# Two layers of cross-attention on one core: early weights behind the next unit's rows, a compact key table, and later copies of value products

## The reference

```
x = attn8(ln(x), ln(x)) + x            # 16 heads of 16; q, k, v and probabilities rounded to 8 bits
x = attn8(ln(x), context) + x          # the same, 77 keys
x = (a * gelu(g)) @ w2 + x             # a, g = halves of ln(x) @ w1, 1024 wide
# second layer
q, k, v = rms(x) @ Wq, rms(context) @ Wk, rms(context) @ Wv    # 16 query heads, 4 key heads of 64
x = softmax(rope(q) rope(k)^T / 8 + mask) v @ Wo + x
x = (silu(x @ Wgate) * (x @ Wup)) @ Wdown + x
```

## Time and profile before

| what | value |
| --- | --- |
| median of 3 runs | 2611.18 us (2611.0 to 2615.15) |
| profiled execution | 2606.43 us |
| its span | 2604.6 us |
| mean granted clock of PE | 0.872 |
| busy: PE, DVE, ACT, POOL | 77%, 69%, 44%, 36% |
| DMA, mean over the span | 96 GB/s |

### The profile page before, as it was taken

How to read it: one execution, slowest core, us unless ns; L and a number is a source line. 1 busy time by engine, 2 the same in 40 slices (tenths; PEclk the granted TensorE clock), 3 DMA queues, 4 the chain that set the end, 5 groups by cost and what they waited for, 6 DMA issues and landing times.

```text
span 2604.6 us, 41636 instructions
## 1 busy us (share of the span) xinstructions
PE 2006.9 (77%) x10552; PEld 1439.3 (55%) x10552; DVE 1807.6 (69%) x3327; ACT 1137.0 (44%) x1906; POOL 944.2 (36%) x1628
## 2 busy tenths in 40 slices
PE   3556477978788787888788787878787787878786
PEld 2323255655556565656556565656555565656665
DVE  1456768677777868677877868677777868685532
ACT  1234453545344553545454554545353545444211
POOL 1213334344443434343443434343433424343212
PEclk8666688999989898998989898998889898989888
DMA  7577453453636353443536363543545353634010
GB/s 234 114 133 145 90 120 73 82 123 75 129 73 133 63 123 74 97 106 74 130 73 132 65 135 61 104 99 74 121 73 124 66 130 60 129 60 105 9 40 4
DMA packets 749785, 251.18 MB, mean 96 GB/s; under 512 B 661244, under 2 KB 742896, under 8 KB 749360
## 3 DMA queue, kind: packets, MB, share of 16 engines
q1 hardware_dynamic: 746287, 249.54, 45.6%
q10 hardware_dynamic: 3328, 0.01, 0.1%
HBM read 88.62 MB, written 22.40 MB: 43 GB/s over the span
## 4 chain that ended last, share of the span: by engine, by line
PE 39%; DVE 18%; issue 16%; SPq 12%; ACT 6%; DMA 5%; POOL 3%; DVEq 1%; ACTq 0%; POOLq 0%
PE work L1389 17%; PE work L1399 14%; SPq L541 4%; DMA PT<-Pn 3%; ACT E L894 3%; DVE scaled_row L1050 3%; PE rowps L1460 3%; DVE Pn L1057 2%; PE outps L1445 2%; DVE hids L1197 1%; POOL scs L794 1%; SPq L532 1%; DVE st L1073 1%; DMA xa<-in_x 1%; DVE xs L1187 1%
## 5 line engine op out<-in xcount | busy, mean ns | idle before, releaser
L1050 DVE TENSOR_SCALAR_CACHE_REDUCE scaled_row<-rowps,der 128x1024 uint8<-128x1024 f32 x512 | 654.6, 1279 | 322.8 <-PE rowps L1460 322.6
L894 ACT ACTIVATE E<-rowps,ebias,der 128x1024 f32<-128x1024 f32 x512 | 615.2, 1203 | 405.0 <-DVE scaled_row L1050 311.4
L1057 DVE TENSOR_SCALAR Pn<-E,rowinv 128x1024 int16<-128x1024 f32 x512 | 390.9, 764 | 164.1 <-DMA PT<-Pn 140.1
L728 POOL TENSOR_TENSOR rowden<-rowsum,raw 128x1 f32<-128x1 f32 x512 | 118.7, 232 | 957.5 <-ACT E L894 956.2
L1460 PE MATMUL rowps<-KC,QP 16*128 16x512 bf16 x1024 | 219.7, 426 | 242.1 <-ACT E L894 232.1
L731 POOL TENSOR_TENSOR rowinv<-rowden,minus 128x1 f32<-128x1 f32 x512 | 332.0, 648 | 91.6 <-POOL rowden L728 91.6
L1460 PEld LDWEIGHTS rowps<-KC,QP 16*128 16x128 bf16 x1024 | 49.0, 92 | 410.6 <-ACT E L894 281.6
L1389 PE MATMUL work<-hTs,ff_w_sb 128*128 128x256 f32 x1024 | 263.8, 413 | 13.0 <-ACT hTs L870 13.0
L1389 PEld LDWEIGHTS work<-hTs,ff_w_sb 128*128 128x128 f32 x1024 | 204.6, 206 | 60.4 <-issue 16.0
L1554 PE MATMUL work<-K,hids 128*128 128x154 f32 x1024 | 156.3, 305 | 28.8 <-DVE scs L1211 18.8
L1554 PEld LDWEIGHTS work<-K,hids 128*128 128x128 f32 x1024 | 141.4, 194 | 46.2 <-DVE scs L1211 25.1
(11 more groups left out here) (142 smaller groups left out, 3281.2 us busy)
## 6 DMA issues: line engine op xcount, KB each, us to landing
VW<-vw_dram SPq DMA_DIRECT2D x32, 640.0 KB, 4.8
K<-k_dram SPq DMA_DIRECT2D x16, 616.0 KB, 4.2
KC<-k_dram SPq DMA_DIRECT2D x128, 64.0 KB, 2.4
VB<-v_dram SPq DMA_DIRECT2D x64, 128.0 KB, 3.2
PT<-Pn SPq DMA_TRANSPOSE x512, 3.1
V<-v_dram SPq DMA_DIRECT2D x16, 320.0 KB, 3.9
vw_dram<-scs SPq DMA_DIRECT2D x32, 154.0 KB
K<-k_dram SPq DMA_DIRECT2D x16, 308.0 KB, 3.1
```

The source lines that it names most:

```text
L728: nc.gpsimd.tensor_tensor(rowden[:, n:n + 1], rowsum[:, n:n + 1], raw[:, DW1:DW1 + 1], ALU.mult).then_inc(row_den.sem, 1)
L894: nc.scalar.activation(E[:, slot, :], rowps[n % 2][:], ACT.Exp, bias=ebias[:, n:n + 1], scale=der[:, AL1:AL1 + 1], accum_out=rowsum[:, n:n ...
L1050: nc.vector.tensor_scalar(scaled_row[:, n % 2, :], rowps[n % 2][:], der[:, NAL1:NAL1 + 1], 3.0e38, ALU.mult, ALU.min, accum_out=ebias[:, n ...
L1057: nc.vector.tensor_scalar(Pn[:, n % 2, :], E[:, ring(n)[0], :], rowinv[:, n:n + 1], 255.0, ALU.mult, ALU.min).then_inc(row_round.sem, 1)
```

## The change

It has three parts.

1. **Order of the early transfers.** `early_sync` yields just behind the load of the next unit's rows (0.05 halves later) instead of 0.3 halves ahead of it or more. All zeros are issued in the first batch. The three small matrices wo, wq2 and wo2 come first, then w1 and w2 behind the second load of rows, and Wq, four small loads and Wgate behind the third.
2. **Compact table of keys.** In memory the table holds each key once (64 rows x 616 columns, 154 KB a batch) and no zeros. So four writes of zeros are left out, and SP has 8 placements in place of 16. The zeros in `K1` itself are written once, by POOL at the end of step 0, after all placements have been read; SP waits for it there. Each unit loads the table with two transfers, one for the upper and one for the lower 64 partitions, in pieces of 77 elements.
3. **Copies of value products.** DVE's and ACT's copies, and SP's stores, are due one half later (+2 and +3 in place of +1 and +2).

```diff
-        k1_dram = dram("k1_dram", (B, P, 2 * KV * 2 * M), F32)
+        k1_dram = dram("k1_dram", (B, HD, 2 * KV * M), F32)
-        k1_in = count("table1_in", 16)
+        k1_in = count("table1_in", 32)
+        PLACED = H + H + 2 * KV
...
             yield 4.5
-            sp.dma_start(K1[:].rearrange("p a g n -> p (a g n)"), k1_dram[bass.ds(b, 1)].rearrange("b p n -> (b p) n")
-                         ).then_inc(k1_in.sem, 16)
+            for pos in range(2):
+                sp.dma_start(K1[HD * pos:HD * pos + HD, :, :, M * pos:M * pos + M],
+                             k1_dram[bass.ds(b, 1)].rearrange("b r (a g k) -> (b r) a g k", a=2, g=KV)).then_inc(k1_in.sem, 16)
...
-            others = matrices(((w1[:], "L0_xattn_ff_w1"), (w2[:], "L0_xattn_ff_w2"), (Wq[:], "L1_xattn_Wq"),
-                               (wo[:], "L0_xattn_a1_wo"), (wq2[:], "L0_xattn_a2_wq"), (wo2[:], "L0_xattn_a2_wo")))
+            others = matrices(((wo[:], "L0_xattn_a1_wo"), (wq2[:], "L0_xattn_a2_wq"), (wo2[:], "L0_xattn_a2_wo"),
+                               (w1[:], "L0_xattn_ff_w1"), (w2[:], "L0_xattn_ff_w2"), (Wq[:], "L1_xattn_Wq")))
...
-                    yield FIRST_EVERY * (i + 1) + 1.5
-                    for b in ((0, 1), (2, 3), ())[i]:
-                        sp.dma_start(k2_dram[b], z16[:, 0:4 * QW]).then_inc(context_zero, 16)
-                        sp.dma_start(v2_dram[b], z16[:, 0:10 * P]).then_inc(context_zero, 16)
-                        sp.dma_start(k1_dram[b], z32[:, 0:4 * QW]).then_inc(context_zero, 16)
-                        sp.dma_start(vw_dram[b].rearrange("(h k) n -> h k n", k=HP)[:, M:HP, :],
-                                     z32[0:H, 0:3 * D]).then_inc(context_zero, 16)
-                    load(others[(0, 1, 3)[i]:(1, 3, EARLY_LOADS)[i]], weights_in)
+                    yield FIRST_EVERY * i + AT["pre"][0][2] + 1.05
+                    if i == 0:
+                        for b in range(B):
+                            sp.dma_start(k2_dram[b], z16[:, 0:4 * QW]).then_inc(context_zero, 16)
+                            sp.dma_start(v2_dram[b], z16[:, 0:10 * P]).then_inc(context_zero, 16)
+                            sp.dma_start(vw_dram[b].rearrange("(h k) n -> h k n", k=HP)[:, M:HP, :],
+                                         z32[0:H, 0:3 * D]).then_inc(context_zero, 16)
+                    load(others[(0, 3, 5)[i]:(3, 5, EARLY_LOADS)[i]], weights_in)
...
                 for g in range(KV):
-                    for pos in range(2):
-                        for cs, src in ((0, krot), (1, kpr)):
-                            yield setup_at(18) + g
-                            c0 = (cs * KV + g) * 2 * M + pos * M
-                            sp.dma_start(k1_dram[:, HD * pos:HD * pos + HD, c0:c0 + M].rearrange("b r k -> r b k"),
+                    for cs, src in ((0, krot), (1, kpr)):
+                        yield setup_at(18) + g
+                        c0 = (cs * KV + g) * M
+                        sp.dma_start(k1_dram[:, :, c0:c0 + M].rearrange("b r k -> r b k"),
...
                 for i in range(VW_ITEMS):
-                    yield setup_at(CONTEXT_ITEMS + i) + 2
+                    yield setup_at(CONTEXT_ITEMS + i) + 3
...
                 beside.rest()
+                if parts["setup"]:
+                    sp.wait_ge(pads, 3)
...
                     nc.gpsimd.memset(pp1.rearrange("p t (h k) -> p (t h) k", k=HP)[:, :, M:HP], 0.0).then_inc(pads, 1)
-                    pool.wait_ge(pads, 2)
+                    pool.wait_ge(setup_placed, 16 * PLACED)
+                    nc.gpsimd.memset(K1_flat, 0.0).then_inc(pads, 1)
+                    pool.wait_ge(pads, 3)
...
                 for i in range(1, VW_ITEMS, 2):
-                    yield setup_at(CONTEXT_ITEMS + i) + 1
+                    yield setup_at(CONTEXT_ITEMS + i) + 2
...
                 for i in range(0, VW_ITEMS, 2):
-                    yield setup_at(CONTEXT_ITEMS + i) + 1
+                    yield setup_at(CONTEXT_ITEMS + i) + 2
```

More of the change, by code:

```diff
@@ L654, in setup_sync @@
                 yield setup_at(9)
-                sp.wait_ge(context_zero, 16 * 4 * B)
+                sp.wait_ge(context_zero, 16 * 3 * B)
                 sp.wait_ge(setup_ready, 1)
@@ L669, in setup_sync @@
                 for g in range(KV):
-                    for pos in range(2):
-                        for cs, src in ((0, krot), (1, kpr)):
-                            yield setup_at(18) + g
-                            c0 = (cs * KV + g) * 2 * M + pos * M
-                            sp.dma_start(k1_dram[:, HD * pos:HD * pos + HD, c0:c0 + M].rearrange("b r k -> r b k"),
-                                         src[HD * (g % 2):HD * (g % 2) + HD, g // 2, :].rearrange("r (b k) -> r b k", b=B)
-                                         ).then_inc(setup_placed, 16)
+                    for cs, src in ((0, krot), (1, kpr)):
+                        yield setup_at(18) + g
+                        c0 = (cs * KV + g) * M
+                        sp.dma_start(k1_dram[:, :, c0:c0 + M].rearrange("b r k -> r b k"),
+                                     src[HD * (g % 2):HD * (g % 2) + HD, g // 2, :].rearrange("r (b k) -> r b k", b=B)
+                                     ).then_inc(setup_placed, 16)
                 for i in range(VW_ITEMS):
-                    yield setup_at(CONTEXT_ITEMS + i) + 2
+                    yield setup_at(CONTEXT_ITEMS + i) + 3
                     h, b = i % 16, i // 16 * 2
@@ L682, in setup_sync @@
                                  vws[:, i % VWS, :, :]).then_inc(vw_stored[i % VWS], 16)
-                sp.wait_ge(setup_placed, 16 * 3 * H)
+                sp.wait_ge(setup_placed, 16 * PLACED)
                 for i in range(VWS):
@@ L1355, in setup_dve_part @@
                     if g == 0:
-                        dve.wait_ge(context_zero, 16 * 4 * B)
+                        dve.wait_ge(context_zero, 16 * 3 * B)
                     empty(nc.vector.tensor_copy(v1T[:, g, :], bank()[:, 0:BM]))
@@ L1548, in high_pe @@
                     if hf == 0 and m == 0:
-                        k1_in.wait(pe, u, 16)
+                        k1_in.wait(pe, u, 32)
                     for e in range(2):
```

## The result

| | before | after |
| --- | --- | --- |
| median, same chip | 2611.09 us (4 runs) | 2569.37 us (4 runs, 2562.45 to 2574.5) |
| ratio | | 0.9838, 95% interval 0.9809 to 0.9867 |
| span of the profiled execution | 2604.6 us | 2565.1 us |
| mean granted clock of PE | 0.872 | 0.876 |
| start of the first score row | 98.28 us | 82.09 us |

The change saves 41.7 us. The forecast was 26.0. The last four lines say where: 16.2 us ahead of step 0, 16.0 in step 0 up to the memset, 2.8 given back by the first rope load (so 29.4 there), and 10.2 more from there to the last one. The prediction had 16.7, 14.5, a loss of 0.8, and in the loop a *loss* of 4.4.

The account below looks back on a forecast made before the run. The loop was taken as bound by work with no one wait to remove, the stretches ahead by queued loads and SP's issues. -16.7 - 5.2 - 9.3 + 0.8 + 4.4 = -26.0 us gives 2585 from the median; range 2567 to 2604.

Parts of the forecast that it names:

- Edit 1: Ahead of step 0: rows issued before weights and zeros start the first score row near 81.5 us, a gain of 16.7.
- good end of 22: Ahead of step 0: gain of 22 us if the full clock from 20 to 34 us speeds each unit's first projection.
- The step that made the value store the next gate: Units 2 and 3: POOL's cast waits for the previous unit's value store behind early loads; transposes at 44.7 and 62.5 us.
- The rival that denied the gate: Ahead of step 0: PE sets the pace, units of about 10.3 us, gain 27 instead of 16.7, 2575 us; chance 0.12.
- Edit 2 in step 0: Step 0: eight placements instead of 16 save 5.2 us on the path; clearing the table at its end loses 0.8.
- Edit 2 in the loop: Table load in 16 units: a second issue costs 0.55 us, on the chain in eight units, 4.4 us lost.
- the good end of 6 us: Table loads in the loop: 6 us given back if bytes alone counted and the queue were the limit.
- half rate for short pieces: Table load: pieces under 512 B at half rate, so 308 KB cost what 616 KB did.
- the slower rival (2626): Table load in 16 units: short pieces land transposes behind it 2.8 us late, +45 less 30.4, 2626 us; chance 0.06.
- Edit 3: Step 0: later value copies cut the product period from 4.15 to 3.5 us, 7.8 saved, plus 1.5 ahead, 9.3.
- the bounds by PE, SP and the two-row loop: Step 0's product period once copies are later: PE 3.1, SP 2.9, two-row loop 2.9 us a row; 3.5 taken.
- The clock's pattern: Loop steps of the same work take 142.4 or 146.8 us; steps changing sides give 2572 or 2598; chance 0.12.

Follow-up runs that it names:

- e1: The kernel before with the new order of early transfers alone, the key table's zeros kept in the first batch: 2599.25 us, ratio 0.9968.
- e2: The kernel before with the compact key table alone: 2580.55 us, ratio 0.9901.
- e8: The changed kernel with the second and third batch of early loads behind the value stores of units 0 and 1: 2555.43 us, ratio 0.9807 to the kernel before.
- e3: The kernel before with the later copies and stores of value products alone: 2601.67 us, ratio 0.9979.
- e4: The changed kernel with the wide table of before, its zeros, 16 placements and one load a unit: 2587.52 us, ratio 0.9931 to the kernel before.
- e6: The changed kernel with two small table loads a unit of 64 pieces each, most of the table not loaded: 2566.02 us, ratio 0.9838 to the kernel before.
- e9: The changed kernel with one small table load a unit of 64 pieces, most of the table not loaded: 2565.89 us, ratio 0.9848 to the kernel before.
- e5: The kernel before with its 616 KB table loaded in two transfers of 64 partitions each: 2611.37 us, ratio 1.0021.
- e12: The changed kernel with 12 already met waits on SP ahead of its loop over the middle steps: ratio 0.9887 to the kernel before.
- e13: The kernel before with 48 already met waits on SP ahead of its loop over the middle steps: ratio 1.0012.

## Why the prediction was right in sign and range, and short in size

**Edit 1: right.** Unit 1's transposes at 29.59 (forecast 30.4), unit 2's at 46.69 (44.7), unit 3's at 62.38 (62.5), the first row at 82.09 (81.5). Unit 2 is 2 us later: SP stood 2.95 us at the issue of unit 0's value store, where one of 0.4 was taken, and from 20 to 34 us the DMA engines moved 343 GB/s, where 403 was taken. Which of the two makes the 2 us was not separated. (The prediction read PE as almost without a gap from 20 to 34 us in the kernel before; it was busy 8.31 of 14 us. Only its good end of 22 rests on that.) Of the 16.2 us, e1 gives 7.3 alone, and the absent zeros of the table 8.7 (e2). The step that made the value store the next gate is shown by e8. The rival that denied the gate was wrong of this kernel and right, to 1 us, of the one without it.

**Edit 2 in step 0: right.** The placements were put at 5.2 us; e2 shows 6.7. The clearing of the table and SP's wait were put at 0.8. From the memset to the first rope load e2 loses 3.2 and the changed kernel 2.8, where e3 and e4, which lack them, lose nothing. In the changed kernel only 0.9 of that lies behind the clearing, as the roundings above show. In e2 the next rounding is at 231.23 against 245.86 us, so 0.8 is lost by then; the other 2.4 go later in step 1, and what takes them was not found.

**Edit 2 in the loop: a term is missing.** The step read "8 x 0.55 = 4.4 us lost", for the second issue. e6 against e9 shows 0.1 us for it, which their spread makes uncertain by several us, e5 at most 0.43%; with the gap put back, e12's profiled loop loses 3.4. Its size may be anything from nothing to the forecast. What failed is that the loop's instructions were taken to be the only thing that the change does to it. The edit takes 12 records off SP's program ahead of the loop and by this lets SP's body stand where the jump leaves no gap: nine jumps of 2.7 us less, of which 12.8 us show in the ratio of e12. That the missing time is an instruction fetch rests on the packets and on the Trainium skill's rule above; that it goes with SP's place ahead of the loop is shown. The profile had it to be read: SP on the chain through its issues in the first 25 us of many steps was SP late from the jump, with 12% of the chain before, 4% after and 11% in e12, and was taken for the price of the issues.

**The pieces.** The rule of 512 B weighed against the good end of 6 us. The prediction's half rate for short pieces was an estimate, and no run shows it: they land in 4.0 us against 4.3. Neither bytes nor pieces reach the time, so the good end and the slower rival (2626) both fall, the good end for another reason than the rule.

**Edit 3: right, with another sharing.** The period is 3.71 and not 3.5, so the twelve periods give 5.3 us and not 7.8 (in e3 it is 3.74, from 168.67 to 213.54). e3 gains 8.7 us in step 0 by its trace (7.9 to the memset, from a first row 0.8 later), where 9.3 was forecast. What is late next is DVE's copy of the bank, which PE waits for at both ends of the stretch; the bounds by PE, SP and the two-row loop, all near 3, left it out. ACT's wait for products did not vanish, it halved, from 40.3 to 18.9 us.

**The sum.** -16.2 - 16.0 + 2.8 = -29.4 against -30.4 up to the loop: right to 1 us, with the loss of 0.8 and the gain of 14.5 in step 0 near the 0.9 and 14.1 that the roundings give. The loop: -10.2 against +4.4. Without the gap's term the forecast fits: e12's ratio times the 2611.2 of the prediction is 2581.7, and 2585 was forecast. With it, 2569 fell inside the range of 2567 to 2604, near its end, and outside the likeliest case's 2576 to 2595. That it fell inside is luck: the range was made for other causes.

**The clock's pattern.** In the profiled executions some steps take about 142 us and some 147, whatever the kernel; in the kernel before those of 142 to 143 us have a granted clock of 0.93 to 0.95, the others 0.90 or 0.91. Of nine steps three are short in the kernel before, four in e3 and one in e13. So e3's loop moved by -6.1 and e13's by +6.7 though neither edit touches the loop's own work, and is the reason why the loop's term rests on the ratios and on the gap itself, not on one trace.

## What to carry to other kernels

In a kernel with a loop on the engines, look at each engine's first instruction behind the jump, and at packets of instructions that start behind it: an edit ahead of the loop can turn this cost on or off, and then its time is not the edit's. Before a cost in a loop is put down to an issue or a transfer, shift the loop by instructions that do nothing. And when loads are moved out of the way of one wait, ask which store stands behind them now: here moving two batches behind the value stores gave 8 to 11 us more.

## What the hardware showed that was not expected

- SP's jump back costs 0.2 us or 2.8 us by where its body stands; six records more ahead of a body of 302 turned one into the other. PE, with a body of over 800 records, and the other engines never paid it.
- SP is late by 2.7 us behind each of nine jumps, 24 us. The profiled execution of e12 is 12.5 us longer than that of the changed kernel.
- The same 616 KB land 4.0 us after the issue in 2048 pieces of 308 B and 4.3 us in 128 pieces of 4928 B, each in two issues, with no difference in the whole time.
- One issue of this load takes 0.34 us of SP for 128 partitions with one long piece each. It takes 0.58 to 0.59 for 64 partitions with one piece each, long or short, and 0.63 to 0.67 for 512 or 1024 short pieces.
